# One W1 load per batch as the stationary operand, and one scaling per pair moved from VectorE to ScalarE and GpSimd

## The reference

```python
h       = relu(x[b] @ W1[id] + b1[id])        # 128x512 @ 512x128
adapted = h @ W2[id] + b2[id]                 # 128x128 @ 128x512
y       = x[b] + adapted
normed  = (y - mean(y)) * rsqrt(var(y) + 1e-5)   # over the 512 features
out[b]  = x[b] + normed * gamma[id] + beta[id]
```

## Time and profile before

| | before |
|---|---|
| time, median of 3 runs | 325.21 us (325.19 to 325.84) |
| span of the profiled execution, first to last instruction | 323.8 us |
| PE busy | 301.9 us (93%) |
| DVE busy | 307.6 us (95%) |
| ACT busy | 230.4 us (71%) |
| POOL busy | 185.7 us (57%) |
| moved by DMA | 75.69 MB, mean 234 GB/s |

### The profile page before, as it was taken

One profiled execution on the slowest core, in us unless ns is written; L12 is line 12 of the kernel. 1 busy time (PEld: TensorE's weight loads), 2 busy tenths in 40 slices (PEclk: granted clock), 3 DMA queues, 4 the chain that ended last, 5 costly groups with the idle time before them and its releaser, 6 DMA issues. The chain is left out here.

```text
span 323.8 us, 8068 instructions
## 1 busy us (share of the span) xinstructions
PE 301.9 (93%) x2200; PEld 272.8 (84%) x2200; DVE 307.6 (95%) x679; ACT 230.4 (71%) x541; POOL 185.7 (57%) x217
## 2 busy tenths in 40 slices
PE   1659999999999999999999999999999999999962
PEld 1239899999999999999999999999999999999941
DVE  5687999999999999999999999999999999999996
ACT  3956677777777777877778777787777877778752
POOL 2960755556655566555665556655566555665553
PEclk9877999999999999999999999999999999999995
DMA  5999988766766667676776676766667666433324
GB/s 160 302 356 428 379 291 273 236 228 231 257 232 227 228 229 263 223 233 226 230 256 232 228 231 227 261 236 221 231 225 262 221 234 232 160 132 134 130 108 152
DMA packets 41711, 75.69 MB, mean 234 GB/s; under 512 B 2253, under 2 KB 7404, under 8 KB 41542
## 3 DMA queue, kind: packets, MB, share of 16 engines
q1 hardware_dynamic: 41571, 75.04, 68.5%
q10 hardware_dynamic: 99, 0.14, 0.1%
HBM read 41.62 MB, written 33.55 MB: 232 GB/s over the span
## 5 line engine op out<-in xcount | busy, mean ns | idle before, releaser
L295 POOL TENSOR_TENSOR x_io<-x_io,beta_all 128x512 f32<-128x512 f32 x128 | 161.2, 1280 | 0.0
L401 PE MATMUL ps_h<-w_all,x_T 128*128 x1024 | 137.0, 284 | 0.0
L401 PEld LDWEIGHTS ps_h<-w_all,x_T 128*128 128x128 f32 x1024 | 126.1, 194 | 1.6
L345 ACT ACTIVATE cut<-ps_y,row_sum 128x512 bf16<-128x512 f32 x128 | 88.0, 688 | 24.0 <-PE ps_y L428 24.0
L572 DVE SCALAR_TENSOR_TENSOR x_io<-ps_y,rstd,x_io 128x512 f32<-128x512 f32 x128 | 90.2, 747 | 2.5 <-DVE rstd L564 0.3
L559 DVE SCALAR_TENSOR_TENSOR ps_y<-ps_y,mean,gamma_all 128x512 f32<-128x512 f32 x128 | 90.8, 754 | 0.8 <-ACT cut L345 0.6
L292 POOL TENSOR_TENSOR mean<-row_sum,over_h 128x2 f32<-128x2 f32 x64 | 12.9, 201 | 125.6 <-DVE ps_y L540 113.6
L540 DVE SCALAR_TENSOR_TENSOR ps_y<-x_io,b_all 128x512 f32<-128x512 f32 x124 | 83.1, 713 | 0.0
L393 PE MATMUL ps_T<-identity,x_io 128*128 128x128 f32 x512 | 68.2, 277 | 10.0 <-DMA x_io<-in_x 10.0
L393 PEld LDWEIGHTS ps_T<-identity,x_io 128*128 128x128 f32 x512 | 61.1, 143 | 19.1 <-issue 10.4
L322 ACT COPY x_T<-ps_T 128x1024 f32<-128x1024 f32 x64 | 63.7, 995 | 8.2 <-PE ps_T L393 8.2
(11 more groups left out here) (60 smaller groups left out, 173.6 us busy)
## 6 DMA issues: line engine op xcount, KB each, us to landing
x_io<-in_x SPq DMA_DIRECT2D x64, 512.0 KB, 4.4
out<-x_io SPq DMA_DIRECT2D x63, 512.0 KB, 3.0
x_io<-in_L_cond_W SPq DMA_DIRECT2D x5, 512.0 KB, 7.2
w_all<-in_L_cond_W SPq DMA_DIRECT2D x5, 512.0 KB, 8.9
b_all<-in_L_cond_b SPq DMA_DIRECT2D x1, 2560.0 KB, 15.7
out<-x_io SPq DMA_DIRECT2D x2, 256.0 KB, 2.0
x_io<-in_L_cond_gamma SPq DMA_DIRECT2D x1, 60.0 KB
x_io<-in_L_cond_beta ACTq DMA_DIRECT2D x1, 60.0 KB
```

What stands on the lines that cost most here:

```text
L295: nc.gpsimd.tensor_tensor(x_slot(t), x_slot(t), of_lang(beta_all, langs[b]), ALU.add)\
L345: nc.scalar.activation(squares[:, t % 2, :], ps_y[t % Y_BANKS][:, :], ACT.Square, scale=-float(H), bias=stat(row_sum, t), accum_out=stat(s ...
L401: last = nc.tensor.matmul(part, x_T[:, t % 4, c, :], w1_all[:, bass.ds(lang, 1), c, :].rearrange("p o a -> p (o a)"), start=False, stop=(c ...
```

## The change

- W1 is no longer resident. SP loads the W1 of each batch by a DMA of its own (256 KB, 2 KB per partition) into a ring of four pairs, `w1_stage`, six pairs ahead of the pair that it stores. To address it, SP loads the language ids of each pair into registers.
- W1 is now the stationary operand and x_T the moving one, so h comes out turned, with A on the partitions. `turn_h`, `copy_h` and `h_rows` go; `high_h` applies the relu and `low_h` reads the same bank. The b1 term is one matmul of 256 columns per pair, from `b1_parts` and a 0/1 table `is_lang`, which is built in the prologue. There are two banks `ps_h` in turn.
- So that W1 can be loaded with contiguous 2 KB, the features are split as 4p + c instead of 128c + p: `turn_x` reads x with a step of four elements.
- `second_product` follows two pairs behind (FIRST = 2) instead of three.
- The second tile of each pair is scaled elsewhere: ACT writes bank minus mean to an SBUF tile `centred`, POOL multiplies it by gamma (`gain`), and DVE finishes it from there, one iteration later. The bank of the second tile is free once ACT has read it.

```diff
+            def stage_w1(q):
+                langs = langs_of(sp, q)
+                if q >= STAGE_PAIRS:
+                    sp.wait_ge(h_summed, q - STAGE_PAIRS + 1)
+                for b in range(2):
+                    sp.dma_start(w1_stage[:, 2 * (q % STAGE_PAIRS) + b, :, :], w1_rows[:, bass.ds(langs[b], 1), :, :])\
+                        .then_inc(w1_staged[q % STAGE_PAIRS], 16)
...
             for p in range(PAIRS - 1):
+                if p + STAGE_AHEAD < PAIRS:
+                    stage_w1(p + STAGE_AHEAD)
                 sp.wait_ge(out_ready, 2 * p + 2)
...
+            def gain(n, lang):
+                pool.wait_ge(centred_ready, n + 1)
+                nc.gpsimd.tensor_tensor(centred[:, n % 2, :], centred[:, n % 2, :], of_lang(gamma_all, lang), ALU.mult)\
+                    .then_inc(gained, 1)
...
             for n in range(PAIRS):
-                add_beta(n)
+                langs[n] = langs_of(pool, n)
+                mean_of_pair(n)
+                add_beta(2 * n, langs[n][0])
+                if n > 0:
+                    gain(n - 1, langs[n - 1][1])
+                add_beta(2 * n + 1, langs[n][1])
+            gain(PAIRS - 1, langs[PAIRS - 1][1])
...
+            def centre(n):
+                t = 2 * n + 1
+                act.wait_ge(adapted, t + 1)
+                act.wait_ge(mean_ready, n + 1)
+                if n >= 2:
+                    act.wait_ge(out_ready, 2 * (n - 2) + 2)
+                nc.scalar.activation(centred[:, n % 2, :], ps_y[t % Y_BANKS][:, :], ACT.Identity,
+                                     bias=stat(neg_mean, t)).then_inc(centred_ready, 1)
...
-                    last = nc.tensor.transpose(ps_T[:, t % 2, c, :], x_io[:, t % SLOTS, c * 128:(c + 1) * 128],
+                    last = nc.tensor.transpose(ps_T[:, t % 2, c, :], x_slot(t).rearrange("s (p c) -> s c p", c=C)[:, c, :],
                                                identity[:, :])
...
+            def first_products(p):
+                bank = pair_of(ps_h[p % 2])
+                if p >= 2:
+                    pe.wait_ge(h_low_ready, p - 1)
+                nc.tensor.matmul(bank.rearrange("a (b s) -> a b s", b=2), b1_parts[:, :],
+                                 is_lang[:, 2 * p:2 * p + 2].unsqueeze(2).broadcast_to([128, 2, S]), start=True, stop=True)
+                pe.wait_ge(w1_staged[p % STAGE_PAIRS], 32 * (p // STAGE_PAIRS + 1))
                 for b in range(2):
+                    for c in range(C):
+                        last = nc.tensor.matmul(bank[:, b * S:(b + 1) * S],
+                                                w1_stage[:, 2 * (p % STAGE_PAIRS) + b, c, :],
+                                                x_T[:, (2 * p + b) % 4, c, :],
+                                                start=False, stop=False, skip_group_check=True)
+                last.then_inc(h_summed, 1)
...
-                    if t >= Y_BANKS:
+                    if t >= Y_BANKS and b == 0:
                         dve.wait_ge(out_ready, t - Y_BANKS + 1)
+                    if t >= Y_BANKS and b == 1:
+                        dve.wait_ge(centred_ready, n - 1)
+                        dve.wait_ge(squared, t - Y_BANKS + 1)
...
+            def finish_second(n):
+                t = 2 * n + 1
+                dve.wait_ge(rstd_ready, n + 1)
+                dve.wait_ge(gained, n + 1)
+                dve.wait_ge(x_beta_ready, t + 1)
+                nc.vector.scalar_tensor_tensor(x_slot(t), centred[:, n % 2, :], stat(rstd, t), x_slot(t),
+                                               ALU.mult, ALU.add).then_inc(out_ready, 1)
...
-            def norm_and_seed(n, p):
+            def norm_and_seed(n):
-                scale_pair(n, langs[n])
+                scale_first(n, langs[n][0])
...
+                if n > 0:
+                    finish_second(n - 1)
                 invert_pair(n)
-                finish_pair(n)
-                if p is not None:
-                    low_h(p)
+                finish_first(n)
                 if n + 2 < PAIRS:
                     seed_pair(n + 2, langs[n + 2])
+                    low_h(n + 2)
```

More of the change, by code:

```diff
@@ L15 @@
 Y_BANKS = 4
-H_PAIRS = 6
-FIRST = 3
+H_PAIRS = 4
+STAGE_PAIRS = 4
+STAGE_AHEAD = 6
+FIRST = 2
 EARLY = 2
@@ L71, in build @@
         b1_parts = sb("b1_parts", [128, A], BF16)
+        count_row = sb("count_row", [128, L], F32)
+        lang_of_row = sb("lang_of_row", [128, 1], F32)
+        is_lang = sb("is_lang", [128, B], BF16)
+        centred = sb("centred", [128, 2, H], F32)
         later_part = sb("later_part", [128, 2], F32)
@@ L89, in build @@
         row_sum = sb("row_sum", [128, SLOTS], F32)
-        mean = sb("mean", [128, SLOTS], F32)
+        neg_mean = sb("neg_mean", [128, SLOTS], F32)
         sq_sum = sb("sq_sum", [128, SLOTS], F32)
@@ L96, in build @@
         ps_T = psum("ps_T", [128, 2, C, S], F32)
-        ps_h = psum("ps_h", [128, H], F32)
-        ps_hT = psum("ps_hT", [128, H], F32)
+        ps_h = [psum(f"ps_h{i}", [128, H], F32) for i in range(2)]
         ps_y = [psum(f"ps_y{i}", [128, H], F32) for i in range(Y_BANKS)]
@@ L106, in build @@
         s_b2 = sem("s_b2")
-        s_w1 = sem("s_w1")
+        w1_staged = [sem(f"w1_staged{i}") for i in range(STAGE_PAIRS)]
         s_w2 = [sem(f"s_w2_{n}") for n in range(W_CHUNKS)]
@@ L116, in build @@
         set_ready = sem("set_ready")
-        over_h_ready = sem("over_h_ready")
+        neg_over_h_ready = sem("neg_over_h_ready")
+        count_row_ready = sem("count_row_ready")
+        lang_of_row_ready = sem("lang_of_row_ready")
+        is_lang_ready = sem("is_lang_ready")
+        centred_ready = sem("centred_ready")
+        gained = sem("gained")
         later_part_ready = sem("later_part_ready")
@@ L217, in load_w2 @@
                     .then_inc(s_w2[n], 16)
[L219 to L223, removed]
+            def stage_w1(q):
[5 more added lines that the diff above has]
+                        .then_inc(w1_staged[q % STAGE_PAIRS], 16)
+            load_w2(0)
+            sp.wait_ge(ids_ready, 1)
+            stage_w1(0)
+            load_w2(1)
             load_x(1)
+            stage_w1(1)
             for n in range(W2_AHEAD, W_CHUNKS):
@@ L234, in _ @@
                 load_x(p)
+            for q in range(STAGE_PAIRS, STAGE_AHEAD):
+                stage_w1(q)
             for n in range(W_CHUNKS):
@@ L354, in step @@
                     copy_x(p + 1)
-                if p > 0:
-                    high_h(p - 1)
-                copy_h(p)
+                high_h(p)
             def copy_spread(n):
@@ L371, in _ @@
             high_w2(2)
-            copy_h(0)
-            copy_x(2)
             high_h(0)
             high_w2(3)
-            copy_h(1)
+            copy_x(2)
+            high_h(1)
             high_w2(4)
-            step(2)
             for p in range(FIRST, PAIRS):
                 square_pair(p - FIRST)
+                centre(p - FIRST)
                 step(p)
-            square_pair(PAIRS - FIRST)
-            high_h(PAIRS - 1)
-            for n in range(PAIRS - FIRST + 1, PAIRS):
+            for n in range(PAIRS - FIRST, PAIRS):
                 square_pair(n)
+                centre(n)
         @block.tensor
@@ L465, in _ @@
                     turn_x(2 * p + 3)
-                if p > 0:
-                    turn_h(p - 1)
-                for b in range(2):
-                    first_product(2 * p + b, langs[p][b])
+                first_products(p)
                 if p < PAIRS - 1:
@@ L551, in seed_early, with scale_first @@
                                                    accum_out=stat(row_sum, t)).then_inc(seeded, 1)
-            def scale_pair(n, langs):
+            def scale_first(n, lang):
+                t = 2 * n
+                bank = ps_y[t % Y_BANKS][:, :]
                 dve.wait_ge(mean_ready, n + 1)
-                for b in range(2):
-                    t = 2 * n + b
-                    bank = ps_y[t % Y_BANKS][:, :]
-                    dve.wait_ge(squared, t + 1)
-                    nc.vector.scalar_tensor_tensor(bank, bank, stat(mean, t), of_lang(gamma_all, langs[b]),
-                                                   ALU.subtract, ALU.mult).then_inc(scaled, 1)
+                dve.wait_ge(squared, t + 1)
+                nc.vector.scalar_tensor_tensor(bank, bank, stat(neg_mean, t), of_lang(gamma_all, lang),
+                                               ALU.add, ALU.mult).then_inc(scaled, 1)
             def invert_pair(n):
```

110 lines of the change are left out of this document (49 added, 61 removed).

## The result

| | before | after |
|---|---|---|
| time, median of 4 runs | 325.23 us | 390.45 us |
| ratio to before, 95% interval | | 1.201 (1.198 to 1.205) |
| span of the profiled execution | 323.8 us | 388.6 us |
| DVE / POOL / PE busy | 307.6 / 185.7 / 301.9 us | 364.4 / 325.0 / 300.3 us |
| moved by DMA | 75.69 MB | 106.61 MB |

The changed kernel is 20% slower. The forecast was 368 us with a range to 395: right in the sign, the mechanism and the range, 22 us short in size.

What follows compares the result with a forecast made beforehand. Before, PE bounds at 4.49 us per pair; after, DVE and POOL taking turns at 5.2. Prologue 35.0, 62 pairs 322.4, last two 7.0, end 2.6: span 367.0, plus 1.4 gives 368 us, range 342 to 395.

Steps and rivals of the forecast that it cites:

- TensorE, 4.2: TensorE's work per pair in the loop: 4.49 less 0.22 and 0.08, about 4.2 us.
- the b1 switch: First products on TensorE: one b1 matmul per pair instead of two saves 0.05 to 0.1 us, taken as 0.08.
- the term taken as 0: Transposes of x on TensorE: reading with a 16-byte step adds nothing; bounds 0 and twice the time.
- the doubling of the rival: Strided transposes of x take twice their 0.11 us: TensorE 5.1 us per pair, 362 us without turns; chance 0.06.
- VectorE's own work, 3.8: VectorE per pair in the loop: 4.46 us less one scaling of about 0.67 leaves 3.8 us.
- The turns: Two-SBUF-input VectorE operations and GpSimd's exclude each other: VectorE holds 0.60 us, an add or gain 1.09; chance 0.74.
- The order within a pair: Assumed loop sequence: second finish, mean, add, first seed, gain, second seed, second add; 5.2 us per pair.
- the predicted chain, 5.22: Alternating VectorE and GpSimd holds in a pair: 0.60, 0.15, 1.09, 0.60, 1.09, 0.60, 1.09; 5.2 us, bounds 4.8 and 5.65.
- The prologue: Before the loop, x no longer queues behind W1: 2.0 us won (bounds 0 and 4), first scaling at 35.0.
- DMA as a bound: Rival: DMA sets the loop's pace, 4.5 us for some 50 pairs, then 4.2; 321 us; chance 0.04.
- The other price, 4.2: DMA time per pair in the loop if all 1.57 MB go at 372 GB/s: 4.2 us.
- The seeds, which a rival left out of the turns: Rival: in the loop only the finish collides; GpSimd takes 4.3 us per pair, 313 us; chance 0.07.

Runs made afterwards that it cites:

- run 9: Kernel of run 1 with ScalarE writing 1/std directly, so VectorE's reciprocal goes: 311.5 us, ratio 0.954; 4.26 us per pair.
- run 2: Kernel before plus only the second tile's centring on ScalarE and gain on GpSimd, low_h ahead of the seeds, W1 resident: 399.9 us, ratio 1.230.
- run 3: Kernel before with one wait more: GpSimd's two adds of beta wait for VectorE's low_h of the next pair: 385.2 us, ratio 1.183.
- run 4: Changed kernel with seeds from pair 2 on reading the bank and x, so one SBUF input, b2 left out: 321.6 us, ratio 0.990.
- run 1: Changed kernel with both tiles scaled and finished on VectorE as before, leaving the W1 part alone: 320.2 us, ratio 0.981.
- run 6: Changed kernel with GpSimd's first add of beta waiting, from pair 2 on, for the second finish of pair n - 2: 380.9 us, ratio 1.169.
- run 5: Changed kernel with the gain on 2 of the 512 columns: 332.5 us, ratio 1.018.
- run 8: Changed kernel with GpSimd's two adds and gain as operations with one tensor input and one value per partition: 360.3 us, ratio 1.108.
- run 7: Changed kernel with low_h ahead of the two seeds instead of behind them: 397.8 us, ratio 1.218.

## Why the prediction was right, and where its size was off

Most of its signs came: the add near 1.6 us, the second seed near 1.7, scaling and first finish unchanged, TensorE waiting about 1 us. Three did not: the second finish was to be unstretched and takes 1.20, GpSimd was to be busy above 90% without waits and is at 84% with 0.69 us of wait per pair, and a pair takes 5.58 us instead of 5.2.

- **TensorE, 4.2.** Measured 4.26, in run 9, where nothing hides it. The two transposes and the b1 switch went as said. The transposes with a step of 16 bytes follow each other in 163.77 - 162.81 = 0.96 for eight against 0.88: the term taken as 0 is 0.08, not the doubling of the rival.
- **VectorE's own work, 3.8.** 5.58 - 0.46 - 1.03 = 4.09. Missing was the wait of DVE for its own first finish before the seed of the same bank: 0.22 us idle, and 163.94 - 162.97 = 0.97 from the one to the other instead of 0.66, so 0.31 in all. Before, low_h stood between the two and hid it. The prediction moved low_h and priced the move at nothing. In run 2, where low_h stands ahead of the seeds, 3.79 is what is left: the 3.8 was right for that order.
- **The turns.** Holds of 0.60 and 1.09 were taken from the prologue; the loop shows 0.60 and 1.10. Runs 3, 4 and 1 show the mechanism from three sides: it comes with the position alone, goes with the second SBUF input alone, and is gone without the detour.
- **The order within a pair: the step that failed.** The prediction put the second finish ahead of the mean and first add. It also put the second add behind the second seed. But the second add starts between the two seeds and is over before the second one is; the mean then waits for that seed (0.69 us idle on GpSimd) and starts as soon as it is done, 0.8 us ahead of the finish, and the add behind the mean holds the finish 0.46. So the bound is not GpSimd's own chain, 5.2, but VectorE with two holds: 4.09 + 0.46 + 1.03 = 5.58. Run 6 put the order back and came to 5.40: the predicted chain, 5.22, and 0.18 for the wait that it takes to enforce the order. So it shows the chain as right for its order; the 0.38 us are the order, not longer holds. 62 x 0.38 = 23.6 us is the miss of the loop, and the rest of the sum is off by little.
- **The prologue.** The first scaling came at 32.9 instead of 35.0: 4.1 us won where 2.0 was taken, at the bound of 4. TensorE now starts at 19.86 instead of 21.67, held by the last copies of the tables, as argued, so 1.8 us were won there. But the first `second_product` comes at 30.91 against 35.01. It waits for the last w2_low in both kernels, and this one ends at 30.78 instead of 34.86; only the bound of 4 had allowed for W2 coming sooner.
- **The rest.** From the last pair with seeds to the end 9.9 us against 9.6; 1.8 us over the span against 1.4. Together: 368.4 + 23.6 - 2.1 + 0.3 + 0.4 = 390.6, measured 390.45.
- **The rivals.** DMA as a bound was priced at 4.5 us per pair from the busy share. Run 9 moves the same bytes at 4.26. A share near 1 was read as full; it was not. The other price, 4.2 by the 372 GB/s of the earlier trace rows, is not contradicted. The seeds, which a rival left out of the turns, are in them (run 3), and the strided transposes cost 0.08, not 0.88.

## What to carry to other kernels

Before moving work to an idle engine, look at when it is idle: GpSimd's 2 us of rest lay exactly under VectorE's two-input operations, and that kept those at their full speed. Look for such a pair of engines in the odd places of a trace (here five operations of the prologue), since a tuned loop may never show the collision. And split a change: one half of this one was worth 2% and the other cost 23%.

## What the runs showed of the hardware

- VectorE with two SBUF inputs against GpSimd with two: strictly in turn. At 128x512 float32 the first holds the other for 0.60 us of its 0.75 and the second for 1.10 us of its 1.28, alternating even when the same engine has its next one ready (run 3). Even a 2-column GpSimd operation waits (0.62 instead of 0.20 us, run 5).
- GpSimd with one tensor input lets VectorE in after 0.48 us of 1.56 (run 8).
- VectorE with one input from SBUF and one from a bank is not held, whether it writes SBUF or a bank: 0.75 and 0.74 us in the changed kernel, seeds at 0.72 in run 4.
- A difference of 0.01 or 0.02 us in arrival decides who is held, and with it 0.1 us per pair (run 7 and run 2 against the changed kernel); a wait more can make the kernel faster (run 6) and a wait less slower (run 7).
- Loads and stores mixed, in pieces of 2 KB, ran at 364 GB/s from 60 to 280 us (run 9); a busy share of 1.00 of the DMA engines at 358 GB/s (run 1) was not their limit.
